# Second cross-attention: where the pairs for the row maxima, the output's multiplication and the pooled chunks stand

## The reference, cut to what matters

```
def _L1_xattn_ref(qkv, y):                      # qkv: layernorm(x), (4, 512, 512); y: ctx_2048, (4, 1601, 512)
    N_HEADS = 16
    bs, width, length = qkv.shape
    ch = width // N_HEADS                       # 32
    q = qkv.reshape(bs * N_HEADS, ch, length)
    k = v = y.reshape(bs * N_HEADS, ch, -1)     # 64 heads, 32 x 1601
    scale = 1.0 / math.sqrt(math.sqrt(ch))
    weight = jnp.einsum('bct,bcs->bts', q * scale, k * scale)
    weight = jax.nn.softmax(weight.astype(jnp.float32), axis=-1).astype(weight.dtype)
    a = jnp.einsum('bts,bcs->bct', weight, v)
    return a.reshape(bs, -1, length)
x = x + jnp.tanh(g_xattn[1]) * _L1_xattn_ref(_layernorm(x, axis=-1), ctx_2048)
```

## Time and profile before

| | us |
|---|---|
| median of 3 runs (lowest, highest) | 1898.48 (1896.98, 1900.62) |
| profiled execution | 1899.03 |
| its span, from the first to the last instruction | 1897.2 |
| busy in the span: PE, PEld | 1623.6, 608.1 |
| busy in the span: DVE, ACT, POOL | 1173.8, 845.8, 825.6 |

### The profile page before, as it was taken

The page is one execution under the profiler, slowest core; times in us unless marked ns, Lnnn a source line. Parts: engine busy times, 40 slices in busy tenths (PEclk is TensorE's granted clock), DMA queues, the critical chain, the costliest instruction groups (busy, mean ns, idle before and its releaser), DMA issues. The chain is left out here.

```text
span 1897.2 us, 22118 instructions
## 1 busy us (share of the span) xinstructions
PE 1623.6 (86%) x7540; PEld 608.1 (32%) x7568; DVE 1173.8 (62%) x1538; ACT 845.8 (45%) x1241; POOL 825.6 (44%) x324
## 2 busy tenths in 40 slices
PE   5999999798778877888888888888888888699898
PEld 2444444343333331222222222222222221244443
DVE  3768999885455547766566666566666650434543
ACT  1221211211443432677776667677667768111111
POOL 0022232543221124767667786566778767100000
PEclk9999999899899995999999999999999999799999
DMA  9231222313111123122221222222122224000000
GB/s 329 81 110 60 81 97 86 103 34 115 56 33 34 34 61 90 55 73 72 73 57 44 58 60 72 74 73 59 40 58 61 55 53 92 1 0 22 22 22 22
DMA packets 136395, 124.36 MB, mean 66 GB/s; under 512 B 61774, under 2 KB 112226, under 8 KB 136294
## 3 DMA queue, kind: packets, MB, share of 16 engines
q1 hardware_dynamic: 131302, 112.56, 21.1%
q10 hardware_dynamic: 4992, 10.49, 1.7%
HBM read 73.49 MB, written 10.76 MB: 44 GB/s over the span
## 5 line engine op out<-in xcount | busy, mean ns | idle before, releaser
L1477 ACT ACTIVATE c_prob<-c_scores,ctx_scales 128x512 f32<-128x512 f32 (+1 forms) x832 | 534.6, 685 | 287.4 <-PE c_scores L1533 279.9
L1384 DVE TENSOR_REDUCE c_piece_max<-c_unit 128x1 f32<-128x804 f32 x512 | 481.4, 984 | 288.6 <-PE c_unit L1516 284.2
L1322 POOL TENSOR_TENSOR c_prob_sum<-c_prob_sum,c_prob 128x2048 f32<-128x2048 f32 x96 | 434.5, 4526 | 23.5 <-ACT c_prob L1477 18.8
L1516 PE MATMUL c_unit<-c_khigh,c_qdiag 128*128 128x402 f16 x1024 | 264.6, 348 | 118.0 <-DVE c_piece_max L1384 103.8
L1533 PE MATMUL c_scores<-c_queries,c_keys 97*128 97x512 f16 (+1 forms) x832 | 299.5, 390 | 21.8 <-ACT c_prob L1477 13.7
L1542 PE MATMUL c_out<-c_prob,c_VT 128*32 128x512 f32 (+1 forms) x1664 | 224.5, 612 | 0.1
L676 PE MATMUL a_S<-a_ctxT,a_xnT 128*128 128x401 f32 x512 | 192.6, 521 | 7.2 <-ACT a_prob L633 3.9
L706 PE MATMUL a_o<-a_ctx,a_probT 128*128 128x512 f32 (+1 forms) x416 | 183.5, 598 | 0.0
L1533 PEld LDWEIGHTS c_scores<-c_queries,c_keys 97*128 97x128 f16 (+1 forms) x832 | 74.4, 98 | 335.4 <-ACT c_prob L1477 290.3
L1516 PEld LDWEIGHTS c_unit<-c_khigh,c_qdiag 128*128 128x128 f16 x1024 | 80.1, 99 | 265.2 <-DVE c_piece_max L1384 209.3
L1322 POOL TENSOR_TENSOR c_prob_sum<-c_prob 128x2048 f32<-128x2048 f32 x16 | 72.5, 4529 | 164.2 <-ACT c_prob L1477 140.0
(11 more groups left out here) (197 smaller groups left out, 1903.2 us busy)
## 6 DMA issues: line engine op xcount, KB each, us to landing
c_k<-in_keys SPq DMA_DIRECT2D x16, 801.0 KB, 6.9
c_keys<-c_khigh SPq DMA_DIRECT2D x128, 100.1 KB, 2.2
a_ctx<-in_ctx SPq DMA_DIRECT2D x12, 1024.0 KB, 6.5
c_VT<-in_values SPq DMA_DIRECT2D x16, 768.0 KB
a_ctxT<-in_ctxT SPq DMA_DIRECT2D x12, 802.0 KB, 4.7
c_keys<-c_krest SPq DMA_DIRECT2D x64, 100.1 KB, 2.2
a_weights<-in_L_ffn_weight SPq DMA_DIRECT2D x3, 1408.0 KB, 14.3
weights_back<-a_weights SPq DMA_DIRECT2D x3, 1408.0 KB, 8.7
```

Of the source, the lines that this page charges most:

```text
L1322: nc.gpsimd.tensor_tensor(psum4[:], a[:], prob[(j * MC + c) % RING][:], ALU.add).then_inc(sums_taken, 2 if i == 1 else 1)
L1384: nc.vector.tensor_reduce(piece_max[j % 2][:, k // 2, k % 2:k % 2 + 1], U[bank(unit)][:, :, 0:PIECE], axis=AX.XY, op=ALU.max).then_inc(uni ...
L1477: nc.scalar.activation(prob[(j * MC + c) % RING][0:w, h, :], STp[h % 2][0:w, :], ACT.Exp, scale=score_scale[0:w]).then_inc(exp_done, 1)
L1516: last = nc.tensor.matmul(U[bank(unit)][:, e, 0:PIECE], QZ[o][:, h, t * P:(t + 1) * P], khigh[o][:, at:at + PIECE], start=True, stop=True)
```

## The change

Three edits, all in `cross_attention_1`. The additions on GpSimd keep their number; the chunks that they take are others, so that SUMMED is 4, 6, 9, 11, 12 and no more 4, 7, 10, 11, 12. GpSimd multiplies and adds the output of the group before behind its fifth addition and no more behind its first, and VectorE's four reciprocals stand before units 3, 5, 7 and 9 of the stream and no more before 3, 4, 5 and 6. TensorE's units are placed by count: a gap with a block gets none, and the units are spread evenly over the gaps without one. The waits themselves are as before.

```diff
-        POOLED = [0, 1, 2, 3, 5, 6, 8, 9]
+        POOLED = [0, 1, 2, 3, 5, 7, 8, 10]
...
                 add_up(g, j, 1)
-                if not isinstance(g, int) or g > 0:
-                    add_gain(g - 1)
                 add_up(g, j, 2)
                 add_up(g, j, 3)
                 add_up(g, j, 4)
                 add_up(g, j, 5)
+                if not isinstance(g, int) or g > 0:
+                    add_gain(g - 1)
                 add_up(g, j, 6)
...
-                    if before and 3 <= u < 3 + PARTS:
-                        finish(g - 1, u - 3)
+                    if before and u in range(3, 3 + 2 * PARTS, 2):
+                        finish(g - 1, (u - 3) // 2)
...
-                BLOCK, PAIR = 1.25, 0.36
-                per_gap = (BLOCK * len(gaps) + PAIR * max(len(stream), UNITS)) / (H * MC)
-                given, done = 0, 0.0
+                free_gaps = H * MC - len(gaps)
+                given = passed = 0
...
                     if what:
-                        done += BLOCK
-                    upto = (gap - 3) * per_gap
-                    while given < len(stream) and (done + PAIR / 2 <= upto or gap == 4 * MC + 3):
+                        return
+                    passed += 1
+                    upto = len(stream) if passed == free_gaps else passed * max(len(stream), free_gaps) // free_gaps
+                    while given < min(len(stream), upto):
                         unit = stream[given]
                         if unit[0] == "rows" and gap < ROWS_GAP:
                             break
                         rows(unit) if unit[0] == "rows" else pair(unit)
                         given += 1
-                        done += PAIR
```

More of the change, by code:

```diff
@@ L1586, in slot @@
                 gaps = placed(before)
-                BLOCK, PAIR = 1.25, 0.36
-                per_gap = (BLOCK * len(gaps) + PAIR * max(len(stream), UNITS)) / (H * MC)
-                given, done = 0, 0.0
+                free_gaps = H * MC - len(gaps)
+                given = passed = 0
                 def products(gap):
-                    nonlocal given, done
+                    nonlocal given, passed
                     what, b = gaps.get(gap, (None, None))
```

## The result

The changed kernel takes 1832.23 us (median of 4 runs, 1830.44 to 1833.38), the kernel before 1897.86 beside it. The ratio is 0.9651, 95% interval 0.9634 to 0.9668. The forecast was 1833.6. The profiled execution took 1832.33, its span 1830.5.

The account below looks back on a forecast made before the run. Bursts of pairs, with TensorE and VectorE waiting for each other through two PSUM buffers, bound the kernel. Passes of 49.9 instead of 54.54 us save 60.3, pass 14 4.6, together 64.9: 1833.6 us, range 1812 to 1864.

Parts of the forecast that it names:

- Prices of the gaps: TensorE, passes 1 to 13: 19 blocks at 1.48 us, 12 lone pairs at 0.41, 7 triples at 2.00; sum 47.0.
- (B): Rival: waits vanish more fully, ScalarE's stall partly hidden, copies land early; 48.6 us a pass, 1816 us; chance 0.13.
- ScalarE's stall before gap 14: Score of gap 14 waits for ScalarE's exponential behind the keys' split, done at 11.5; 2.0 us, 2.2 with gaps 10 to 12.
- VectorE: Maxima, reciprocals and small work take 35.1 us in 49, so there is room; 0.3 added for late pairs, giving 49.5.
- The loop through gap 30: GpSimd's rests, then SyncE's copies, feed the next pass's gap 30 pair; hidden or 50.1 us a pass, 49.9 taken.
- The gain behind the fifth addition and the other pooled chunks: GpSimd's 4.15 us wait for the last reciprocal goes; later additions and rests shift, and no probability tile in the ring waits.
- Passes 14 and 15: Pass 14 saves 4.6 us (bounds 2 and 6); pass 15, without pairs, saves 0 (bounds -1 and +1).
- Pass 0: 49 units on 35 free gaps, VectorE near its limit either way; change 0 us, bounds -2 and +2.
- (A): Rival: the loop through gap 30 is longer than summed, 2 us more per pass; 51.9 a pass, 1860 us; chance 0.20.
- (D): Rival: nothing moves, the loop or ScalarE holds the pass near 54.5 us; 1898 us; chance 0.04.
- (C): Rival: VectorE never empties before a triple, each pair waits a whole maximum; 55.5 us a pass, 1912 us; chance 0.05.
- The marks: Signs of being right: passes 49 to 51 us, pairs' waits on maxima below 40, gap 30's pair waiting below 1.

Follow-up runs that it names:

- Even pairs alone: Kernel before with only the stream's units placed by count, one in each gap without a block; 1836.03 us, ratio 0.9661.
- the second experiment: Kernel before with only the gain moved behind the fifth addition and reciprocals before units 3, 5, 7, 9; 1908.34 us, ratio 1.0038.
- the rests early: Kernel after with GpSimd's rests of queries and keys before its fifth addition, not at the pass's end; 1829.63 us, ratio 0.9645.
- keys apart and rests early: Kernel after with ScalarE's key scaling behind chunk 3, rounding behind chunk 5, and GpSimd's rests before the fifth addition; 1795.50 us, ratio 0.9466.
- the keys apart alone: Kernel after with ScalarE's key scaling behind chunk 3 and rounding behind chunk 5, both formerly behind chunk 2; 1811.60 us, ratio 0.9553.

## Why the prediction was right, step by step

- Prices of the gaps: right. 1.48, 0.41 and 2.00 stand in the trace after, and with the two later stalls taken away the pass is 47.2 against the sum's 47.0. Reading three prices off gaps that already had the wanted content carried the forecast. That pass has TensorE's row busy for 45.4 of 47.24 us, 96%, the share that (B)'s 48.6 was said to need. The row is no fixed floor either: the 46.9 of before are 45.4 here for the same work.
- ScalarE's stall before gap 14: right, 11.56 into the pass against 11.5 worked out; the term of 2.2 measured 1.9. Taking it away, and the loop with it, brought 37 us in the medians. Of the 39.2 in the profiled spans, 31.9 lie in passes 1 to 13; 4.6 are the last stage, which no edit touched.
- VectorE: right that there is room; 0.3 was too much. The plain passes are 49.0 to 49.1 where the sum was 49.5.
- The loop through gap 30: right in kind, wrong in weight. I took 49.9 for it; in the kernel after it holds passes 6 and 11, 1.3 us together, and moving the rests alone changes nothing. The landing was under-sized: 4.9 is the median of 64 copies and not the most. In the pass shown it took about 4.7 behind the end of the issue. The links ahead of it were over-sized: the rests are done 49.4 into a pass and not 50.1, SyncE starts 0.2 behind them and not 0.8, and its issues take 19.9 and not 21.2. So the diagonal is there 1.0 before gap 30.
- A term I did not have: in four passes TensorE ran at 1.2 GHz for a while behind the stall of gap 13 (last section), about 6.4 us together. The forecast for passes 1 to 13 was 714.1 - 60.3 = 653.8, with the 5.1 left in; measured are 651.9. The two passes at the loop's turn are 5.5 over the plain ones, about what I had left. Against the plain pass of 49.1 the forecast put 5.2 for the loop, where there were 1.3, and 5.7 more than was needed for VectorE and ScalarE; it put nothing for the clock, where there were 6.4. So the total came out close partly by luck: a loop that hardly was there, and a clock that was.
- The gain behind the fifth addition and the other pooled chunks: priced at nothing beyond the loop, and undone one by one they are worth nothing.
- Passes 14 and 15: 4.3 together against 4.6. Pass 14 alone gave 5.2; pass 15 is 1.0 longer, and it has a stretch at half the clock that stood in pass 14 before.
- Pass 0: mis-sized. The forecast was 0, between -2 and +2, because VectorE was held to be near its limit there. It was busy for 44.96 of 61.58 us, 73%, and the pass became 3.6 shorter. Even pairs alone make it 58.7, and the kernel with the gain and reciprocals moved alone has 61.7: the placing of the pairs did this too. The other 1.7 ahead of pass 1 lie before pass 0, where no edit stands, and the kernels on record differ by up to 3.7 there. These 5.3 and the last stage's 5.1 the other way cancel in the total, which is luck.
- Rivals: (A), (B) and (D) did not come about; (B)'s 48.6 needed the ScalarE stall gone. (C), a pair that waits for a reciprocal in front of it, is real, but where the pairs come in bursts: the second experiment shows it. I had put it to the wrong kernel.
- The marks: pairs' loads wait 50.5 us for maxima, over the 40 that I had named. The mark was badly set: 7 triples in 13 passes are the 91 waits, 0.56 each, and this 0.56 is part of the price of 2.00. The pair of gap 30 was to wait below 1 us; in pass 11 it waited 1.2.

## What to carry to other kernels

Where two engines wait for each other through two buffers, space the producer's work by what the consumer takes, one unit in each gap that has no other work; price the new order from gaps that the trace already has with that content. Then follow each other engine's queue through the same stretch, because the stall that goes is the cover of the next one (here the bursts' 7.3 us a pass came back only as 5.4, since 1.9 went to a 3.1 us piece on ScalarE), and split the long piece at once. A wait that nothing on the path depends on can stay: GpSimd's 3 to 4 us a pass cost nothing, and moving the multiplication and the reciprocals by themselves made the kernel 0.4% longer.

## What the runs showed of the hardware

The granted clock fell behind a short idle time, in some passes. One pass of the kernel after in three stretches: to the score of gap 14, the 5.3 us behind it, the rest (columns as in the earlier trace rows, the third number from the end is the granted clock):

```profile
1008.32:1019.88 11.56, 9.17 (x55) 2.41 (x54) 8.87 (x10) 10.86 (x16) 7.21 (x3) 1.00 0.40 94
1019.88:1025.20 5.32, 5.32 (x24) 1.16 (x24) 2.86 (x3) 3.07 (x5) 5.16 (x2) 0.68 0.47 108
1025.20:1058.99 33.79, 32.48 (x198) 9.33 (x194) 23.78 (x29) 24.12 (x38) 26.97 (x12) 1.00 0.17 54
```

The score of gap 14 starts behind 1.86 us of TensorE's idle time:

```profile
1019.88 0.39 PE L1533 MATMUL c_scores<-c_queries,c_keys 97*128 97x512 f16 x1 [1.86 <-ACT c_prob L1477]
```

Then part of the next stretch ran at 1.2 GHz (0.68 in the mean), and the pass took 50.7 in place of 49.1. A view from within that part, where TensorE has no idle time at all:

```profile
1022.00:1024.50 2.50, 2.50 (x12) 0.63 (x12) 1.51 (x2) 1.38 (x2) 2.34 (x2) 0.50 0.47 112
```

Other passes with the same stall kept 2.4 GHz throughout, as the one in the result's first view. Four of the 13 passes lost the clock in the kernel after, eight with even pairs alone, eight with the gain and reciprocals as before, six with the rests early; what decides it no run shows. With the stall gone (keys apart and rests early) no pass of the 13 has such a stretch but the one at the turn of the loop. With the keys apart alone pass 4 has one too, behind a wait of 2.2 us in gap 30. A stall of 1.9 us thus cost about 3.5 in four passes.

At the turn of the loop TensorE stands still for 2.7 to 3.7 us in every kernel here. In the kernel after the wait is 3.14 us, for nothing that the profile shows, and the granted clock falls behind it too (0.50 from 1162 to 1168):

```profile
1160.30 0.10 PEld L1533 LDWEIGHTS c_scores<-c_queries,c_keys 97*128 97x128 f16 x1 [3.14 <-issue]
```

The two passes around it are 5.5 us longer than two plain ones; no experiment removes the turn.
